# Two mixers on one core: where the norm's sum of squares is formed, and when its column product is issued

## The chip, the cores and the metric

The kernel runs on one core of a Trainium2 chip. The metric is the device time of one execution in microseconds (us), lower is better; the time before is the median of 3 runs. Engines are named as the profile names them: PE is TensorE (PEld its weight loads), DVE VectorE, ACT ScalarE, POOL GpSimd, SP the queue that issues most transfers.

## What is computed

`x` is (4, 1024, 512) float32, 4096 tokens of 512 features. Four residual stages follow each other, each on a layer norm of its input: mixer A, a feed-forward stage, mixer B, the same feed-forward stage again. Both mixers are state-space layers. Cut to what matters here, one of them is:

```
proj = x @ W_in                       # z (1024 wide), x/B/C (convolved over 4 taps, silu), dt
y    = scan over time per head, + D * x     # in tiles of 128 tokens, all in matmuls
A:  yf = y * silu(z);  out = (yf * rsqrt(mean(yf*yf) + eps) * norm_w) @ W_out
B:  out = (y * rsqrt(mean(y*y) + eps) * norm_w * silu(z)) @ W_out
```

The mean goes over the 1024 features of a token. Mixer A has 16 heads of width 64 and a state of 64, mixer B 64 heads of width 16 and a state of 128.

## The kernel before

`mixer_phase` is built once for each mixer. A step (a supertile in the code) is 256 tokens, two tiles of 128; there are 16 steps, 13 of them in a hardware loop. `FOLD` is true for mixer A alone (`2 * N == P`), and `NP` is 1 in A and 4 in B.

Features lie on the partitions: `yz[:, k, :]` holds features 128k to 128k+127 of a tile's 128 tokens, k from 0 to 7. The output is `yz` times `W_out`: 8 products of 128x512 that add up in one bank (L829). The norm's factor belongs to a token, so it is applied to the finished output (`out_add`, L1440), and what it needs is made in four parts:

- ACT squares `yz` (A) or the y bank (B) in two halves into `sq` (`square`, L1049).
- PE multiplies the eight blocks of `sq` by a matrix of ones (steps `rs0`, `prs`, L819): two products add up in each quarter of a bank's rows. DVE copies the bank to `rs` (`square_sums`, L1426).
- PE multiplies `rs` by the column `quad_row` (steps `rt0`, `prt`, L823): 128 sums, one for each token, in one column. DVE turns them into the variance (`rms_var`, L1430).
- ACT takes logarithm and exponential (`out_rsqrt`), and DVE adds a Newton step (`out_scale`, L93 to L95).

The even tile of a step does all that in the step's middle (`rs0`, `rt0`, `out0`); the odd tile's part is done in the head of the next step (`prs`, `prt`, `pout`), and the last odd tile's in an epilogue.

The order of each engine's work is written out by hand. For PE it is a list of names (`head`, `schedule`), and `run` issues them in turn. Every name that is no `seg`, `ydiag`, `ident` or `xT` uses one of the two `work` banks, alternately in the order of the list, and before it starts, `freed` waits until whoever reads the use two places before it is done:

```
if idx >= 2:
    freed(pe, sec.uses[idx - 2], i, n)
```

Around the change that means: `yoff0a/b` and `yoff1a/b` (L841, L845 in A, L800 in B: the part of y from the state) fill the two banks, DVE empties them in two operations (`from_state`, L1384), and the second of the two must be done before the output product in the bank of `yoffb` may start. `xnT0`, `xnT1` (L754) transpose the normalized x of the step after the next and are copied by ACT (`xnT_copy`, L958); `ident0` (L906) adds y1 to the y bank; `small1` (L791) makes exponents, `dt` (L759) needs both copies. After `pout`, DVE's `out_add` frees the bank for the use two places on. DVE's and ACT's orders are in their `supertile` functions. POOL adds the skip term to y1 after `from_state` (L1659), scales x (`xw`, L1670) and the state (L1676).

## Time and profile before

| what | value |
|---|---|
| median of 3 runs | 2761.14 us (2760.09 to 2762.21) |
| the profiled execution's own time | 2760.65 us |
| its span, first to last instruction | 2758.9 us |
| PE busy | 2678.3 us, 97% |
| DVE, ACT, POOL busy | 1962.0, 1530.8, 905.1 us |
| mean granted TensorE clock | 0.987 of full speed |

Mixer A takes the time from the start to about 1087 us, mixer B that from about 1300 to 2557 us, the two feed-forward stages the rest. The profile's times in a timeline are from the span's start. An fp32 product is two matmul instructions, so that a timeline counts 16 where the code has 8. Matmuls are pipelined: the time that a product takes in a stream is the distance from its start to the next one's, and the printed duration is longer. What bounds a stage is read from PE's idle time inside it and from the wait that ended it.

### The profile page before, as it was taken

What the parts mean: (1) busy time and instruction counts of PE and PEld (TensorE: products, weight loads), DVE (VectorE), ACT (ScalarE), POOL (GpSimd) and SP (SyncE); (2) the same over time, 40 slices, a digit from 0 to 9 for tenths busy, and PEclk for the clock granted to TensorE, in tenths of its full rate; (3) what the DMA queues carried; (4) which work ended last, traced back from release to release, by engine and by line L of the source; (5) the groups of instructions that cost most, each with busy time, mean ns of one, the idle gap of its engine ahead of it and who ended that gap; (6) DMA issues with size and microseconds to landing.
All of it is one profiled execution on the core that took longest, in us unless ns stands there. A gap on an engine that the chain in (4) does not pass through costs nothing. (4 is left out here: it accounts for less than half of the span.)

```text
span 2758.9 us, 49906 instructions
## 1 busy us (share of the span) xinstructions
PE 2678.3 (97%) x17452; PEld 1837.3 (67%) x17452; DVE 1962.0 (71%) x3701; ACT 1530.8 (55%) x2450; POOL 905.1 (33%) x611
## 2 busy tenths in 40 slices
PE   8999999999999999999999999999999999997998
PEld 7777777777777775356776666766677666773454
DVE  5666666666666655297788888888888888876377
ACT  4444444445444453343577677666677767765332
POOL 2222222223322223142333443334433344333144
PEclk8999999999999999999999999999999999998999
DMA  4000000000000005245000000000000000003433
GB/s 130 24 24 23 23 23 23 23 23 23 23 23 27 27 16 207 96 164 212 12 24 23 23 23 15 23 23 23 8 23 23 23 23 19 12 22 129 155 132 138
DMA packets 79994, 139.57 MB, mean 51 GB/s; under 512 B 17958, under 2 KB 17958, under 8 KB 78892
## 3 DMA queue, kind: packets, MB, share of 16 engines
q1 hardware_dynamic: 70812, 125.92, 13.1%
q10 hardware_dynamic: 9104, 12.63, 1.3%
q8 instruction: 47, 0.77, 0.1%
q14 instruction: 31, 0.25, 0.0%
HBM read 104.98 MB, written 33.55 MB: 50 GB/s over the span
## 5 line engine op out<-in xcount | busy, mean ns | idle before, releaser
L730 PE MATMUL work<-b_xnT,shared_w 128*128 128x256 f32 x2304 | 529.9, 384 | 1.9 <-DVE b_parts L1355 0.8
L730 PE MATMUL work<-a_xnT,shared_w 128*128 128x256 f32 x2176 | 497.4, 385 | 1.3
L730 PEld LDWEIGHTS work<-b_xnT,shared_w 128*128 128x128 f32 x2304 | 428.8, 190 | 76.4 <-issue 17.0
L730 PEld LDWEIGHTS work<-a_xnT,shared_w 128*128 128x128 f32 x2176 | 410.5, 191 | 70.3 <-issue 12.3
L1395 DVE TENSOR_TENSOR b_decay<-b_decay,b_gt 128x1024 f32<-128x1024 f32 x256 | 349.2, 1395 | 72.2 <-ACT b_decay L1039 71.6
L1032 ACT ACTIVATE b_decay<-seg 128x1024 f32<-128x1024 f32 x256 | 252.2, 1025 | 192.4 <-PE seg L872 184.5
L1624 POOL TENSOR_TENSOR b_rhs<-b_l_side,of_head 128x1024 fp32r<-128x1024 f32 x32 | 99.1, 3096 | 588.7 <-DVE b_l_side L1364 588.7
L1039 ACT ACTIVATE b_decay<-b_decay 128x1024 f32<-128x1024 f32 x256 | 263.6, 1066 | 0.0
L1659 POOL TENSOR_TENSOR a_y<-a_y,a_skip 128x1024 f32<-128x1024 f32 x32 | 90.0, 2813 | 473.1 <-DVE a_y L1384 473.1
L1274 DVE SCALAR_TENSOR_TENSOR shared_cv<-shared_pre,a_conv_w,shared_cv 128x256 f32<-128x256 f32 x432 | 189.8, 483 | 59.5 <-ACT shared_cv L974 53.8
L829 PE MATMUL work<-a_w_out,a_yz 128*128 128x512 f32 x512 | 228.4, 599 | 3.4 <-DVE a_y L1384 3.4
L829 PE MATMUL work<-b_w_out,b_yz 128*128 128x512 f32 x512 | 229.0, 600 | 0.5
L980 ACT COPY shared_z<-work 128x256 f32<-128x256 f32 (+1 forms) x192 | 84.6, 441 | 261.0 <-PE work L730 260.8
L1274 DVE SCALAR_TENSOR_TENSOR shared_cv<-shared_pre,b_conv_w,shared_cv 128x256 f32<-128x256 f32 x480 | 214.6, 481 | 18.0 <-ACT shared_cv L974 10.6
L973 ACT COPY shared_pre<-work 128x256 f32<-128x256 f32 x304 | 115.4, 380 | 165.5 <-PE work L730 165.5
L1395 DVE TENSOR_TENSOR a_decay<-a_decay,a_gt 128x1024 f32<-128x1024 f32 x64 | 137.9, 2175 | 84.2 <-ACT a_decay L1039 83.7
L829 PEld LDWEIGHTS work<-a_w_out,a_yz 128*128 128x128 f32 x512 | 95.4, 191 | 112.9 <-issue 108.1
L829 PEld LDWEIGHTS work<-b_w_out,b_yz 128*128 128x128 f32 x512 | 95.5, 192 | 110.4 <-issue 108.5
L886 PE MATMUL y<-b_decay,b_xdt 128*32 128x128 f32 x4096 | 129.4, 278 | 6.8 <-DVE b_decay L1395 6.7
L1659 POOL TENSOR_TENSOR b_y<-b_y,b_skip 128x1024 f32<-128x1024 f32 x32 | 82.9, 2590 | 154.3 <-DVE b_y L1384 154.3
L886 PEld LDWEIGHTS y<-b_decay,b_xdt 128*32 128x32 f32 x4096 | 107.9, 111 | 34.7 <-issue 21.8
L1881 PE MATMUL y<-f_x1T,shared_pre 128*128 128x512 f32 x256 | 123.6, 609 | 0.0
(330 smaller groups left out, 4563.6 us busy)
## 6 DMA issues: line engine op xcount, KB each, us to landing
x_mid<-mixer_x_res SPq DMA_DIRECT2D x64, 256.0 KB, 2.0
shared_x<-in_L_attn_a_x SPq DMA_DIRECT2D x16, 512.0 KB, 3.5
mixer_x_res<-in_L_attn_a_x SPq DMA_DIRECT2D x32, 256.0 KB, 2.6
shared_w<-in_L_ffn_d_w SPq DMA_DIRECT2D x2, 4096.0 KB, 13.5
f_d_w<-in_L_ffn_d_w SPq DMA_DIRECT2D x2, 4096.0 KB, 14.9
f_x_res<-x_mid SPq DMA_DIRECT2D x8, 1024.0 KB, 5.7
shared_x<-x_mid SPq DMA_DIRECT2D x16, 512.0 KB, 4.0
mixer_x_res<-x_mid SPq DMA_DIRECT2D x32, 256.0 KB, 2.6
```

The costliest lines, as they stand in the source:

```text
L730: mm = nc.tensor.matmul(dst, w_in[:, k, col:col + m], xnT[:, k, :], start=(k == 0), stop=(k == KD - 1))
L829: mm = nc.tensor.matmul(bank[:, :], yz[:, k, :], w_out[:, k, :], start=(k == 0), stop=(k == KE - 1))
L886: mm = nc.tensor.matmul(ybank[32 * q:32 * q + 32, slot * P:(slot + 1) * P], xdt[:, j, 4 * slot + q, 16 * odd:16 * odd + 32], decay[:, slot ...
L973: nc.scalar.copy(pre[0:m, b, HALO:], bank[0:m, 0:SUP])
L980: nc.scalar.copy(z_raw[:, got[0]:got[-1] + 1, :], sec.bank(name)[:, 0:len(got) * SUP].rearrange("p (b t) -> p b t", t=SUP)).then_inc(z_rea ...
L1032: nc.scalar.activation(decay[:, slot_buffer(j, s)].rearrange("p h l -> p (h l)"), seg[s % 2][:, :], ACT.Relu, scale=-1.0).then_inc(seg_tak ...
L1039: nc.scalar.activation(d, d, ACT.Exp, scale=-1.0).then_inc(exp_done, 1)
L1274: ins = nc.vector.scalar_tensor_tensor(out=cv[0:m, b, :], in0=pre[0:m, b, t:t + SUP], scalar=conv_w[0:m, b, t:t + 1], in1=cv[0:m, b, :], o ...
L1395: nc.vector.tensor_tensor(d, d, gt[:, j].unsqueeze(1).to_broadcast([P, 8, P]), ALU.mult).then_inc(m_ready, 1)
L1624: nc.gpsimd.tensor_tensor(rhs[1][:], l_side[:, 1].unsqueeze(1).to_broadcast([P, 8, P]), c["of_head"][:].unsqueeze(2).to_broadcast([P, 8, P ...
L1659: nc.gpsimd.tensor_tensor(y1[:], y1[:], skip[:], ALU.add).then_inc(y1x_ready, 1)
L1881: mm = nc.tensor.matmul(ybank[:, (m % 2) * 512:(m % 2 + 1) * 512], gate_w[:, k, m * P:(m + 1) * P], x1T[n][:, k, :], start=(k == 0), stop= ...
```

## The change

- Mixer A: the eight products with ones and DVE's copy are gone (`rs0`, `prs`). DVE adds the eight blocks of `sq` itself, with one reduction that reads `sq` with the block as the innermost axis (`add_squares`), and `rt0`, `prt` use a column of ones.
- Both mixers: `rt0` is no longer issued ahead of `out0`, but inside it, after the second of its eight products. In mixer A `prt` goes inside `pout` in the same way; in mixer B it stays where it was. The order of the bank uses is kept, so `out0` still waits for the second part of `from_state`.
- Mixer A, head of a step: PE's order after `seg0.0` was `prt, xnT0, pout, xnT1, ident0, small1` and is now `pout (prt inside), xnT0, ident0, xnT1, small1`. ACT squares the odd tile first of all instead of after `bt_copy`, and copies `xnT0` after the second exponential. DVE's reduction comes first, and `rms_var` after the second `make_xdt`.

```diff
@@ head(prev, nxt)
-                    + (["prs"] if prev else []) + ["yoff0a", "yoff0b", "seg0.0"] + (["prt"] if prev else [])
-                    + (["xnT0"] if nxt else []) + (["pout"] if prev else [])
-                    + (["seg0.1"] if NP > 1 else []) + (["xnT1"] if nxt else [])
-                    + ["ident0", "small1"])
+                    + (["prs"] if prev and not FOLD else []) + ["yoff0a", "yoff0b", "seg0.0"]
+                    + (["prt"] if prev else []) + (["xnT0"] if nxt and not FOLD else []) + (["pout"] if prev else [])
+                    + (["seg0.1"] if NP > 1 else []) + (["xnT0", "ident0"] if nxt and FOLD else [])
+                    + (["xnT1"] if nxt else []) + ([] if nxt and FOLD else ["ident0"]) + ["small1"])
@@ schedule, the part for NP == 1
-            steps += ["rs0", "yoff1a", "yoff1b", "seg1.0", "rt0", "out0"]
+            steps += ["yoff1a", "yoff1b", "seg1.0", "rt0", "out0"]
...
-        epi_steps = ["prs", "prt", "pout"]
+        epi_steps = ["prt", "pout"] if FOLD else ["prs", "prt", "pout"]
@@ use(name, sec)
-                        mm = nc.tensor.matmul(bank[:, 0:1], rs[:], c["quad_row"][:], start=True, stop=True)
+                        column = ones[:, 0:1] if FOLD else c["quad_row"][:]
+                        mm = nc.tensor.matmul(bank[:, 0:1], rs[:], column, start=True, stop=True)
...
                         for k in range(KE):
+                            if k == KE // 4 and (name == "out0" or FOLD):
+                                use("rt0" if name == "out0" else "prt", sec)
                             mm = nc.tensor.matmul(bank[:, :], yz[:, k, :], w_out[:, k, :],
@@ run(sec, steps)
-                            use(name, sec)
+                            if name != "rt0" and not (FOLD and name == "prt"):
+                                use(name, sec)
@@ ScalarE, supertile
+                    if prev and FOLD:
+                        square(2 * i - 1)
                     z_copy(sec, "zza")
...
-                    if prev:
+                    if prev and not FOLD:
                         square(2 * i - 1)
...
-                    if nxt:
+                    if nxt and not FOLD:
                         xnT_copy(sec, 0)
                     slot_exp(sec, 0, 1)
+                    if nxt and FOLD:
+                        xnT_copy(sec, 0)
@@ VectorE
+                def add_squares(tile):
+
+                    dve.wait_ge(sq_done, FREE + 2 * (tile + 1))
+                    nc.vector.tensor_reduce(rs[:], sq[:].rearrange("p b t -> p t b"), mybir.AxisListType.X, ALU.add
+                                            ).then_inc(rs_ready, 1)
@@ VectorE, supertile
+                    if prev and FOLD:
+                        add_squares(2 * i - 1)
                     masked_gt(sec)
                     make_xdt(sec, 0)
-                    if prev:
+                    if prev and not FOLD:
                         square_sums(sec, "prs")
                     from_state(sec, 0)
-                    if prev:
+                    if prev and not FOLD:
                         rms_var(sec, "prt")
                     make_xdt(sec, 1)
+                    if prev and FOLD:
+                        rms_var(sec, "prt")
...
-                    square_sums(sec, "rs0")
+                    add_squares(2 * i)
                     from_state(sec, 1)
```

PE, the head of a step of mixer A (`a_sq` squares, `a_state`/`a_bcs` the part from the state, `a_rs` the sums, `shared_x` the transposes `xnT`, `a_y` the product `ident0`, `a_aa` `small1`, `a_xnT` with 128x16 `dt`). Before:

```order
L819 MATMUL work<-a_sq,ones 32x128 x8
L841 MATMUL work<-a_state,a_bcs 128x256
L845 MATMUL work<-a_state,a_bcs 128x256
L841 MATMUL work<-a_state,a_bcs 128x256
L845 MATMUL work<-a_state,a_bcs 128x256
L872 MATMUL seg<-a_rhs,a_lhs 128x512 x4
L823 MATMUL work<-quad_row,a_rs 128x1
L754 MATMUL work<-ident,shared_x 128x128 x4
L829 MATMUL work<-a_w_out,a_yz 128x512 x8
L754 MATMUL work<-ident,shared_x 128x128 x4
L906 MATMUL y<-ident,a_y 128x128 x8
L791 MATMUL work<-tri_le,a_aa 64x128 x2
```

The same place in the changed kernel, whose lines are numbered a little higher:

```order
L844 MATMUL work<-a_state,a_bcs 128x256
L848 MATMUL work<-a_state,a_bcs 128x256
L844 MATMUL work<-a_state,a_bcs 128x256
L848 MATMUL work<-a_state,a_bcs 128x256
L875 MATMUL seg<-a_rhs,a_lhs 128x512 x4
L832 MATMUL work<-a_w_out,a_yz 128x512 x2
L824 MATMUL work<-ones,a_rs 128x1
L832 MATMUL work<-a_w_out,a_yz 128x512 x6
L754 MATMUL work<-ident,shared_x 128x128 x4
L909 MATMUL y<-ident,a_y 128x128 x8
L754 MATMUL work<-ident,shared_x 128x128 x4
L791 MATMUL work<-tri_le,a_aa 64x128 x2
```

The products with ones are gone, the column product sits inside the output products, the first transposes have moved behind these, and `ident0` stands ahead of the second transposes, which are now next to `small1`.

DVE, the same head. Before:

```order
L1345 TENSOR_TENSOR a_gt<-work,tri_le 128x256
L1328 TENSOR_TENSOR a_xdt<-a_xt,a_dt 128x1024
L1426 COPY a_rs<-work 128x128
L1384 TENSOR_TENSOR a_y<-work,a_e 128x512 x2
L1430 TENSOR_SCALAR a_rv<-work 128x1
L1328 TENSOR_TENSOR a_xdt<-a_xt,a_dt 128x1024
L1395 TENSOR_TENSOR a_decay<-a_decay,a_gt 128x1024
```

In the changed kernel:

```order
L1439 TENSOR_REDUCE a_rs<-a_sq 128x128
L1353 TENSOR_TENSOR a_gt<-work,tri_le 128x256
L1336 TENSOR_TENSOR a_xdt<-a_xt,a_dt 128x1024
L1392 TENSOR_TENSOR a_y<-work,a_e 128x512 x2
L1336 TENSOR_TENSOR a_xdt<-a_xt,a_dt 128x1024
L1444 TENSOR_SCALAR a_rv<-work 128x1
L1403 TENSOR_TENSOR a_decay<-a_decay,a_gt 128x1024
```

The copy became a reduction that waits for ACT alone and stands first; what follows `from_state` is now `make_xdt`, then the variance.

PE, the middle of a step of mixer B (`b_state` the part from the state, `b_w_out` the output products), in the changed kernel:

```order
L800 MATMUL work<-b_state,b_bcs 128x512 x2
L875 MATMUL seg<-b_rhs,b_lhs 128x512 x4
L832 MATMUL work<-b_w_out,b_yz 128x512 x2
L824 MATMUL work<-quad_row,b_rs 128x1
L832 MATMUL work<-b_w_out,b_yz 128x512 x6
```

Before, the row with `b_rs` stood between `seg` and the eight output products; nothing else moved there.

## Rows read from the trace of the kernel before

**Rows 1.** Busy time by engine in mixer A's and mixer B's loops (start:end, length, PE, PEld, DVE, ACT, POOL, clock, DMA).
```profile
120.00:880.00 760.00, 748.70 (x4361) 547.06 (x4360) 487.79 (x1010) 368.62 (x662) 221.91 (x136) 1.00 0.07 24
1400.00:2300.00 900.00, 897.10 (x6984) 629.68 (x6984) 743.56 (x1224) 639.92 (x966) 334.65 (x165) 1.00 0.06 20
```
**Rows 2.** Timeline of PE, middle of a step of mixer A (start us, length us, ...).
```profile
486.33 0.64 PE L819 MATMUL work<-a_sq,ones 128*32 128x128 f32 x16
486.90 0.70 PE L841 MATMUL work<-a_state,a_bcs 64*128 64x256 f32 x2
...
488.88 0.38 PE L823 MATMUL work<-quad_row,a_rs 128*128 128x1 f32 x2
489.48 1.98 PE L829 MATMUL work<-a_w_out,a_yz 128*128 128x512 f32 x4 [0.21 <-DVE a_y L1384]
```
**Rows 3.** Timeline of DVE at the same place.
```profile
487.04 0.29 DVE L1426 COPY a_rs<-work 128x128 f32<-128x128 f32 x1 [1.92 <-PE work L819]
488.14 1.29 DVE L1384 TENSOR_TENSOR a_y<-work,a_e 128x512 f32<-128x512 f32 x2 [0.80 <-PE work L841]
```
**Rows 4.** Timeline of ACT at the same place.
```profile
484.56 1.23 ACT L1049 ACTIVATE a_sq<-a_yz 128x512 f32<-128x512 f32 x2 [3.69 <-DVE a_yz L1420]
...
486.44 0.37 ACT L980 COPY shared_z<-work 128x256 f32<-128x256 f32 x1 [0.39 <-PE work L730]
```
**Rows 5.** Timeline of PE, head of the next step of mixer A.
```profile
515.75 0.65 PE L819 MATMUL work<-a_sq,ones 128*32 128x128 f32 x16
...
519.47 7.03 PE L829 MATMUL work<-a_w_out,a_yz 128*128 128x512 f32 x16
526.34 0.60 PE L754 MATMUL work<-ident,shared_x 128*128 128x128 f32 x4
526.77 1.04 PE L906 MATMUL y<-ident,a_y 128*128 128x128 f32 x8
527.89 0.44 PE L791 MATMUL work<-tri_le,a_aa 128*64 128x128 f32 x4
528.26 1.96 PE L759 MATMUL work<-shared_w,a_xnT 128*128 128x16 f32 x16
530.07 2.19 PE L730 MATMUL work<-a_xnT,shared_w 128*128 128x256 f32 x9
```
**Rows 6.** DVE's reductions over 128 and over 64 elements, by source line.
```profile
L332 DVE TENSOR_REDUCE of_head<-hd x1: 286/286/286, 6.6 to 6.6; 128x8 f32<-128x128 f32 x1
L333 DVE TENSOR_REDUCE low_row<-low x1: 210/210/210, 6.8 to 6.8; 128x1 f32<-128x64 f32 x1
```
**Rows 7.** Timeline of DVE in the same head.
```profile
517.55 1.29 DVE L1384 TENSOR_TENSOR a_y<-work,a_e 128x512 f32<-128x512 f32 x2 [0.80 <-PE work L841]
...
522.85 2.35 DVE L1395 TENSOR_TENSOR a_decay<-a_decay,a_gt 128x1024 f32<-128x1024 f32 x1 [2.80 <-ACT a_decay L1039]
...
527.10 0.74 DVE L1440 SCALAR_TENSOR_TENSOR mixer_x_res<-work,a_rr,mixer_x_res 128x512 f32<-128x512 f32 x1
```
**Rows 8.** Timeline of POOL in the same head.
```profile
522.21 1.90 POOL L1670 TENSOR_TENSOR a_xw<-a_xdt,a_e 128x1024 f32<-128x1024 f32 x1
```
**Rows 9.** Timeline of ACT in the same head: the copy of the second transposes.
```profile
526.97 0.59 ACT L958 COPY a_xnT<-work 128x512 f32<-128x512 f32 x1 [2.49 <-PE work L754]
```
**Rows 10.** Timelines of ACT and DVE, last step of mixer A and its epilogue.
```profile
1058.63 1.23 ACT L1049 ACTIVATE a_sq<-a_yz 128x512 f32<-128x512 f32 x2 [7.65 <-DVE a_yz L1420]
...
1062.65 1.29 DVE L1384 TENSOR_TENSOR a_y<-work,a_e 128x512 f32<-128x512 f32 x2 [1.65 <-PE work L841]
...
1086.34 2.94 ACT L232 ACTIVATE shared_z<-shared_z,ffn_shift,ffn_r_in 128x512 f32<-128x512 f32 x4 [5.74 <-POOL ffn_shift L226]
```
**Rows 11.** Timelines of PE and DVE, middle of a step of mixer B.
```profile
1915.33 0.38 PE L823 MATMUL work<-quad_row,b_rs 128*128 128x1 f32 x2
1915.75 7.13 PE L829 MATMUL work<-b_w_out,b_yz 128*128 128x512 f32 x16
...
1915.00 0.69 DVE L1384 TENSOR_TENSOR b_y<-work,b_e 128x512 f32<-128x512 f32 x1 [0.17 <-PE work L800]
```

More of the change, by code:

```diff
@@ L1611, in _ @@
                 sec = epilogue()
-                square_sums(sec, "prs")
+                if FOLD:
+                    add_squares(2 * NSUP - 1)
+                else:
+                    square_sums(sec, "prs")
                 rms_var(sec, "prt")
```

## The prediction

> **What bounds the kernel now.** I read first the busy time by engine inside the two mixers' loops [rows 1]: PE works 748.7 of 760 us in mixer A and 897.1 of 900 us in mixer B, at a granted clock of 1.00, while DVE, the next one, is at 488 and 744 us. So what counts is the start of each PE product, and the question at every edit is whether a removed or moved product leaves PE working or waiting. That is read from the timelines around the output products, one step of each mixer, since the steps of a loop repeat.
>
> In the middle of a step of A [rows 2] the products with ones hold PE for 486.90 - 486.33 = 0.57 us. Then come the part from the state, `seg`, and the column product at 488.88. The output products start at 489.48, after 0.21 us of idling that DVE's second y1 ended: it ran 488.14 + 1.29 = 489.43 [rows 3]. Remark this: **the output product waits for y1, and the column product before it is done inside that wait**. In mixer B it is the same to the hundredth, though the profile prints no idle time there: the second y1 ends at 1915.00 + 0.69 = 1915.69, the output products start at 1915.75, and the column product at 1915.33 fills the 0.42 us before [rows 11].
>
> **What the change costs and gives, part by part.**
>
> *The price of a column product in the stream.* Inside the output products nothing covers it but its first weight load. The nearest row is `dt`, 16 instructions with only 16 columns and full weights, from 528.26 to 530.07 [rows 5]: 0.113 us each, so 0.23 us for the two of a column product. The bounds are 0.1 (only one of the two loads shows) and 0.42 (what it takes alone, [rows 11]). I take 0.23, because the operation is the same and the streams alike.
>
> *DVE's reduction.* It reads 1024 elements. Reductions over 128 and over 64 elements took 0.286 and 0.210 us [rows 6]: 0.0012 us an element, so 0.29 + 896 x 0.0012 = 1.35 us. An operation over 2 x 512 elements took 1.29 [rows 3]. I take 1.3; the bounds are 1.1 and, because these rows read neighbouring elements and the new one jumps 512 bytes from element to element, twice the estimate, 2.6.
>
> *Even tile of A.* The squares end at 484.56 + 1.23 = 485.79 [rows 4], so the reduction runs 485.85 to 487.15, where DVE idled 1.92 us for PE [rows 3]. On PE the part from the state moves to 486.33. Its second product needs the other bank, now freed by ACT's copy at 486.44 + 0.37 = 486.81 [rows 4] instead of by DVE's copy at 487.04 + 0.29 = 487.33 [rows 3]. That is 0.52 us earlier, and with it go `seg` and both y1: the first y1 would start at 487.62, and the reduction is done before. The output products start 0.52 earlier and take 0.23 more: **-0.29 us**. The 0.57 us of products is thus given back almost by half, since the column product leaves its cover. 15 such tiles: -4.4 us.
>
> *Odd tile of A, in the next head.* Again everything up to y1 moves up by 0.53, from 518.84 to 518.31 [rows 7]. ACT's squares and DVE's reduction are done before the head's first products end. The output products start at 518.36; they took 526.34 - 519.47 = 6.87 [rows 5], and 0.23 more now, to 525.46. `xnT0` adds 0.43 and `ident0` 0.9 (the printed 1.04 is pipelined, the transposes go at 0.11 to 0.12 an instruction), to 526.8. Now `xnT1` stands in the place two behind `pout` and waits for DVE's `out_add`, as `small1` did before. In the old trace `out_add` ended at 527.10 + 0.74 = 527.84 and `small1` started at 527.89 [rows 5, 7]: DVE's chain was the bound there already. What sets it: the first slot product of DVE took 2.35 us, although 1.2 is enough; it ended at 525.20, 1.1 us after POOL's `xw` at 522.21 + 1.90 = 524.11 [rows 7, 8]. Whatever the reason, DVE came through when POOL was done, and POOL's chain starts from y1, 0.5 us earlier now. So `out_add` ends about 0.55 earlier, 527.25. `xnT1` starts at 527.30, 0.5 us late. And behind it there is only `small1` to cover ACT's copy: before, that copy began 526.97 - 526.34 = 0.63 after the transposes' start and took 0.59 [rows 9]. So `dt` starts at 527.30 + 0.63 + 0.59 + 0.05 = 528.57, against 528.26 [rows 5]: **+0.31 us**. 14 heads: +4.4 us. The first step's head has no `pout`, but `dt` also comes behind the later `xnT1`: +0.5, once.
>
> *Last step of A.* PE has no projections left there, and the chain runs over the squares, the sums and y1. The squares end at 1058.63 + 1.23 = 1059.86; with a reduction of 1.3 y1 starts at 1061.2 instead of 1062.65 [rows 10]: -1.45. Its head gives another -0.3. Behind the epilogue, the next stage waits for ACT's normalization, 1086.34 + 2.94 = 1089.28 [rows 10], which hangs on DVE's last Newton step; 0.57 us of products and a copy of 0.29 with their handovers are exchanged for 1.3 us of reduction: 0.
>
> *Mixer B.* The output product still waits for the second y1, so it starts at 1915.75 as before, and the column product now costs its 0.23 inside. **+0.23 us** for each of 16 even tiles, PE being full: +3.7. `rms_var` comes 1.7 us later, but ACT, which waits for it, has two exponentials to do first.
>
> Sum: -4.4 + 4.4 + 0.5 - 1.45 - 0.3 + 0 + 3.7 = **+2.4 us** on the profiled execution's own 2760.65, which lies 0.49 under the median of the runs. On the median: 2761.14 + 2.4 = **2763.5 us**. About 0.2%, 5.5 us, is what a measurement of this kernel can tell from no change.
>
> **The rivals.**
>
> *The reduction is slow.* It may take up to 1.8 us before y1 of the even tile is late (487.62 - 485.85). At 2.6 it costs 0.8 in each of 15 even tiles, and 1.3 each in the last step and the epilogue: +14.6, so 2778. For it speaks only that no row reads with such a jump; against it, that the rows of DVE, whatever they read, are all near 1.2 ns an element.
> The Trainium skill ("SBUF — State Buffer", in the section "Door 1: The DMA port swizzle") says that each access to a new 16-byte line pays a penalty, so that float32 can be strided only 4 elements for free; every element of this reduction is on a new line. No row here shows it; if it holds for VectorE, this rival is the outcome.
>
> *The head is worse: DVE's chain does not move up with POOL.* Then `out_add` still ends at 527.84, `xnT1` starts at 527.89 and `dt` at 529.16: +0.9 instead of +0.31, 14 times, +8.3 more: 2771.8, slower. It decides from an `out_add` that moves less than 0.3 us. For it: the slot product also waits for ACT's exponential, whose start the change doesn't move.
>
> *The head is free.* If `out_add` ends by 526.8, `dt` is bound by the transposes alone and starts at about 528.05: -0.2 instead of +0.31, 14 times, -7.1: 2756.4, just inside no change. DVE would have to gain a full microsecond.
>
> *PE's busy time is what counts.* Removed are 32 x 0.57 = 18.2 us of an engine that is 98 to 99% busy; if the waits I found give way too, nearly all of it comes back: 2761 - 18 + 4 = 2747. Against it stands that each of these products is followed by a wait for y1 [rows 2], which the change only shifts.
>
> **How the numbers follow.** Forecast 0.52, slow reduction 0.08, worse head 0.16, free head 0.14, full gain 0.10. Of the forecast's share I give 0.04 to slower, 0.03 to faster, since +-0.25 us in one head is +-3.5 us, and 0.1 to 0.42 for the column product is another -4 to +6; of the free head's 0.05 is faster. So faster 0.18, slower 0.28, same 0.54. The range runs from the free head to the worse one, 2756 to 2771.8, and leaves out the slow reduction and the full gain, 0.18 together.
>
> **What would show it.** In the new profile: the reduction at 1.2 to 1.4 us; the output products of A's even tile starting within 0.1 us of the end of y1; a column product of 0.2 to 0.25 us between the second and third output product; in A's head an idle time of some 0.5 us before the second transposes, ended by `mixer_x_res` of DVE, and another of 0.2 to 0.4 before `dt`, ended by ACT's copy; a step of A as long as before, a step of B 0.23 us longer. The prediction is wrong if a step of A is shorter by more than 0.3 us, or if the time of B does not grow.

## The result, and the profile after

The changed kernel takes **2784.02 us** (median of 4 runs, 2783.32 to 2784.55); the kernel before, run beside it, 2761.68 (2760.09 to 2763.30). The ratio is 1.008, 95% interval 1.0064 to 1.0096: slower by 0.8%, where I had forecast 2763.5 and a range up to 2771.8. The profiled execution's span is 2782.8 us, against 2758.9.

Busy time by engine in the two loops, changed kernel, the columns of [rows 1]:
```profile
120.00:880.00 760.00, 734.50 (x3896) 533.08 (x3895) 492.49 (x977) 363.39 (x645) 231.61 (x136) 0.98 0.07 24
1400.00:2300.00 900.00, 893.53 (x6962) 625.47 (x6961) 741.99 (x1217) 640.78 (x959) 336.23 (x166) 1.00 0.06 21
```
Mixer B looks as before. In mixer A PE is busy 14 us less; since both windows are 760 us long, that says that it waits 14 us more, not that it has 14 us less to do. Beside it **the granted clock is 0.98 instead of 1.00**. To see where, I took the distance from one step's `sums` products (three small ones, issued once in a step) to the next one's (start to start, us):
```
            before                  changed kernel
mixer A     58.78, then 14 x 65.87  59.54, 66.09, 67.76, 67.78, 67.77, 66.09, 67.77, 67.78,
                                    66.08, 67.76, 67.77, 67.77, 66.08, 67.77, 67.70
mixer B     74.33, 76.68,           77.36, 76.92,
            12 x 76.80, 77.47       12 x 77.02, 77.71
```
Every step of A is 0.22 us longer, and 10 of the 14 another 1.68 us (the expectations below say 11; it is 10). Two neighbouring heads of the changed kernel in PE's timeline show what the 1.68 us are:
```profile
402.06 1.93 PE L759 MATMUL work<-shared_w,a_xnT 128*128 128x16 f32 x16 [0.40 <-ACT a_xnT L962]
403.84 15.79 PE L730 MATMUL work<-a_xnT,shared_w 128*128 128x256 f32 x72
...
468.15 1.93 PE L759 MATMUL work<-shared_w,a_xnT 128*128 128x16 f32 x16 [0.40 <-ACT a_xnT L962]
469.93 17.47 PE L730 MATMUL work<-a_xnT,shared_w 128*128 128x256 f32 x72
```
The same 72 projections take 15.79 us behind one head and 17.47 behind the next. The windows of 10 us behind these two heads have the clock in the third column from the right:
```profile
404.00:414.00 10.00, 10.00 (x47) 8.81 (x48) 5.81 (x17) 4.67 (x12) 0.00 (x0) 1.00 0.09 24
...
470.00:480.00 10.00, 10.00 (x40) 8.52 (x40) 4.11 (x13) 3.82 (x10) 0.00 (x0) 0.83 0.08 25
471.00:473.00 2.00, 2.00 (x6) 1.56 (x6) 0.76 (x4) 0.06 (x1) 0.00 (x0) 0.50 0.06 20
```
PE is busy in all of both, but in the second the clock is 0.83 on average: a part of it ran at the lower level, 1.2 GHz (the last row, 0.50), the rest at 2.4, and 17% of 10 us are lost, which is the 1.7 us. Such a stretch is called a *fall* from here on. All ten begin 1.8 to 2.8 us behind the start of `dt`, in the first microsecond of the projections. What PE did in the 60 us before, waits and all, is the same to 0.02 us in both.

**The balance of the 24 us of span**, from the starts of the `sums` products:

- mixer A's steps: 14 x 0.22 = +3.1; 10 falls x 1.68 = +16.8; the first step +0.76; what comes before it -1.67; last step and epilogue -0.76. Together +18.1: the next stage starts at 1107.67 instead of 1089.58.
- the stage between gives 0.4 back.
- mixer B: 14 x 0.22 and 0.24 in the last step, +3.2 with rounding; and its first step +3.0.

The last is not the change's. PE waits long in that step in both kernels, and the clock falls there in both (0.84 from 1321 to 1345 before, 0.67 from 1352 to 1373 in the changed one), but where it falls varies. In the kernels below, some of which have B exactly as before, the same step took 74.68 to 77.4 us; the 74.33 of before is the lucky end of that. The -1.67 ahead of A's first step isn't the change's either: the work up to there is the same in all these kernels, and it ended between 42.9 and 45.9 us. Nor is the +0.76 of the first step shown to be: it took 59.40 in the kernel with the reduction alone below, whose head is the old one. So of the 24 us 17 are falls behind A's heads, 3 and -1.7 are chance, and the rest is some 6.

PE's timeline of the changed kernel at the two places of [rows 2, 5], even tile and head:
```profile
493.74 0.70 PE L844 MATMUL work<-a_state,a_bcs 64*128 64x256 f32 x2
...
496.38 1.98 PE L832 MATMUL work<-a_w_out,a_yz 128*128 128x512 f32 x4 [0.55 <-DVE a_y L1392]
498.21 0.28 PE L824 MATMUL work<-ones,a_rs 128*128 128x1 f32 x2
498.35 5.40 PE L832 MATMUL work<-a_w_out,a_yz 128*128 128x512 f32 x12
503.58 3.62 PE L730 MATMUL work<-a_xnT,shared_w 128*128 128x256 f32 x16
...
522.88 0.70 PE L844 MATMUL work<-a_state,a_bcs 64*128 64x256 f32 x2
...
525.50 1.98 PE L832 MATMUL work<-a_w_out,a_yz 128*128 128x512 f32 x4 [0.53 <-DVE a_y L1392]
...
532.70 0.60 PE L754 MATMUL work<-ident,shared_x 128*128 128x128 f32 x4
533.13 1.04 PE L909 MATMUL y<-ident,a_y 128*128 128x128 f32 x8
534.51 0.65 PE L754 MATMUL work<-ident,shared_x 128*128 128x128 f32 x4 [0.34 <-DVE mixer_x_res L1454]
535.09 0.44 PE L791 MATMUL work<-tri_le,a_aa 128*64 128x128 f32 x4
535.93 1.93 PE L759 MATMUL work<-shared_w,a_xnT 128*128 128x16 f32 x16 [0.40 <-ACT a_xnT L962]
537.70 7.54 PE L730 MATMUL work<-a_xnT,shared_w 128*128 128x256 f32 x26
```
There are now four waits in a step: 0.55 and 0.53 ahead of the output products, 0.34 ahead of the second transposes, 0.40 ahead of `dt`. And DVE's and ACT's rows there, which answer to [rows 3, 7, 9]:
```profile
493.23 1.91 DVE L1439 TENSOR_REDUCE a_rs<-a_sq 128x128 f32<-128x1024 f32 x1 [0.70 <-ACT a_sq L1053]
495.05 1.28 DVE L1392 TENSOR_TENSOR a_y<-work,a_e 128x512 f32<-128x512 f32 x2
...
533.64 0.74 DVE L1454 SCALAR_TENSOR_TENSOR mixer_x_res<-work,a_rr,mixer_x_res 128x512 f32<-128x512 f32 x1
...
535.20 0.59 ACT L962 COPY a_xnT<-work 128x512 f32<-128x512 f32 x1 [1.28 <-PE work L754]
```

### The profile page after: what moved, and what is told of

Read it like the earlier page. It is cut to its first block and busy times, and to the rows that moved or that the text cites. A ratio compares the mean times of both kernels' runs of the same rounds, so it can differ in the third digit from the quotient of the medians.

```text
span 2782.8 us, 48759 instructions
## 1 busy us (share of the span) xinstructions
PE 2675.2 (96%) x16940; PEld 1833.7 (66%) x16940; DVE 1995.6 (72%) x3701; ACT 1533.0 (55%) x2450; POOL 916.4 (33%) x611
## 5 line engine op out<-in xcount | busy, mean ns | idle before, releaser
L730 PE MATMUL work<-a_xnT,shared_w 128*128 128x256 f32 x2176 | 513.2, 394 | 1.3
L730 PEld LDWEIGHTS work<-a_xnT,shared_w 128*128 128x128 f32 x2176 | 421.6, 197 | 75.0 <-issue 12.3
L832 PE MATMUL work<-a_w_out,a_yz 128*128 128x512 f32 x512 | 237.0, 607 | 20.4 <-DVE a_y L1392 19.5
L1403 DVE TENSOR_TENSOR a_decay<-a_decay,a_gt 128x1024 f32<-128x1024 f32 x64 | 117.2, 1852 | 38.0 <-ACT a_decay L1043 35.9
```

The lines of the kernel that those rows point to most:

```text
L730: mm = nc.tensor.matmul(dst, w_in[:, k, col:col + m], xnT[:, k, :], start=(k == 0), stop=(k == KD - 1))
L832: mm = nc.tensor.matmul(bank[:, :], yz[:, k, :], w_out[:, k, :], start=(k == 0), stop=(k == KE - 1))
L1403: nc.vector.tensor_tensor(d, d, gt[:, j].unsqueeze(1).to_broadcast([P, 8, P]), ALU.mult).then_inc(m_ready, 1)
```

## The experiments

Three theories. T1: the clock falls because PE waits in A's new head, and what counts is where it waits. T2: it falls with the reduction, or because PE has less to do. T3: it has nothing to do with the waits. The kernel before ran beside each batch, at 2761 to 2762; ratios are against it. Step lengths are of mixer A unless said.

### One part undone at a time

**Head order back.** The changed kernel, with the head's order of before on PE, which also puts the head's column product ahead of `pout` again (the one inside `out0` stays):
```diff
-                    + (["prt"] ...) + (["xnT0"] if nxt and not FOLD else []) + (["pout"] if prev else [])
-                    + (["seg0.1"] ...) + (["xnT0", "ident0"] if nxt and FOLD else [])
-                    + (["xnT1"] ...) + ([] if nxt and FOLD else ["ident0"]) + ["small1"])
+                    + (["prt"] ...) + (["xnT0"] if nxt else []) + (["pout"] if prev else [])
+                    + (["seg0.1"] ...) + (["xnT1"] if nxt else []) + ["ident0", "small1"])
...
-                            if k == KE // 4 and (name == "out0" or FOLD):
-                                use("rt0" if name == "out0" else "prt", sec)
+                            if k == KE // 4 and name == "out0":
+                                use("rt0", sec)
...
-                            if name != "rt0" and not (FOLD and name == "prt"):
+                            if name != "rt0":
```


> The changed kernel with TensorE's order in mixer A's head put back (column product, first transposes, output products, second transposes, ident0, small1); the reduction and the column product inside out0 stay. In the changed kernel a step of A takes 66.09 us, or 67.77 us where the granted clock falls behind dt (11 of 14 steps). Theory 1 (the head's new waits, 0.33 us ahead of the second transposes and 0.40 us ahead of dt, together with 0.53 us ahead of the output products, let the clock fall): with two of the three waits gone no step shows a lower clock, and a step takes 65.87 - 0.28 (even tile) - 0.53 (head) = 65.06 us; the whole some 2752 us. Theory 2 (the reduction on VectorE or the 0.54 us wait in the even tile is what lets the clock fall): most steps keep a fall, 1.7 us each, and the whole is some 2770 us. Theory 3 (the fall has nothing to do with TensorE's waits): the number of falls stays at 11.

Measured: 2761.81 us, ratio 0.9999 (0.9990 to 1.0009). All 14 steps took 65.64 or 65.65, none fell; B 77.02 a step. So with the old head the falls are gone, and 22 us with them. The step is 0.6 longer than expected, for a wait I had not seen. PE's timeline of this kernel:
```profile
516.76 0.65 PE L754 MATMUL work<-ident,shared_x 128*128 128x128 f32 x4 [0.22 <-DVE a_y L1392]
517.88 7.13 PE L832 MATMUL work<-a_w_out,a_yz 128*128 128x512 f32 x16 [0.47 <-DVE a_rv L1444]
```
`pout` waited for `rms_var`, which the change put behind `make_xdt` on DVE. That wait of 0.47 us, longer than `dt`'s 0.40 in the changed kernel, brought no fall.

**Columns ahead.** The changed kernel, with the column products in their own place again, in both mixers:
```diff
                         for k in range(KE):
-                            if k == KE // 4 and (name == "out0" or FOLD):
-                                use("rt0" if name == "out0" else "prt", sec)
...
-                            if name != "rt0" and not (FOLD and name == "prt"):
-                                use(name, sec)
+                            use(name, sec)
```


> The changed kernel with the column products of both mixers ahead of the output products again; the reduction and the new head order stay. Mixer B: a step goes back from 77.02 to 76.80 us in any theory that prices the column product at 0.22 us in the stream and at nothing in the wait for y1. Mixer A: the even tile gains 0.22 us, the head nothing, since it is bound by out_add; a step without a fall of the clock takes 65.87 us. Theory 1: the waits ahead of the output products shrink from 0.53 to 0.2 us, but the one ahead of the second transposes grows to 0.55 us; fewer falls than 11, some 2761 to 2770 us. Theory 3: 11 falls, 2776 us.

Measured: 2775.79 us, ratio 1.0051 (1.0034 to 1.0068). B 76.80 a step, that is 0.22 less than in the changed kernel; A 65.87 without and 67.55 with a fall, 8 falls. The waits ahead of the output products shrink to 0.21, those in the head stay (0.56 and 0.40), and so do most falls. The time is T3's number, but with 8 falls and not 11; T1's range, up to 2770, was missed.

**The reduction alone.** The kernel before, with only the reduction in place of the products with ones, and ACT's squares early in the head; the column products stay ahead, the head's order and `rms_var`'s place stay old:
```diff
-            steps += ["rs0", "yoff1a", "yoff1b", "seg1.0", "rt0", "out0"]
+            steps += ["yoff1a", "yoff1b", "seg1.0", "rt0", "out0"]
...
-                    square_sums(sec, "rs0")
+                    add_squares(2 * i)
... (the same for the odd tile and the epilogue, with the column of ones and the early squares)
```


> The kernel before with the reduction on VectorE in place of the products with ones in mixer A, ScalarE's early squares included, and nothing else: column products ahead, head's order as before. Theory 1: no fall of the clock; both tiles gain what y1 gains, 0.5 us each, so a step of A takes 64.8 us, and the whole some 2746 us: faster than before. Theory 2 (the reduction itself, or the lower share of work on TensorE, lets the clock fall): 1.7 us for each step with a fall, up to 2765 us. Mixer B as before, 76.80 us a step.

Measured: **2748.07 us, ratio 0.9951 (0.9934 to 0.9968), faster than before**. All 14 steps took 64.90 (the last 64.83), no fall; B 76.80. PE does as little here as in the changed kernel, with the same reduction: T2 falls. Its timeline in the even tile and the head:
```profile
482.93 7.13 PE L830 MATMUL work<-a_w_out,a_yz 128*128 128x512 f32 x16 [0.21 <-DVE a_y L1387]
...
512.39 7.03 PE L830 MATMUL work<-a_w_out,a_yz 128*128 128x512 f32 x16
519.26 0.60 PE L754 MATMUL work<-ident,shared_x 128*128 128x128 f32 x4
519.69 1.04 PE L907 MATMUL y<-ident,a_y 128*128 128x128 f32 x8
520.88 0.44 PE L791 MATMUL work<-tri_le,a_aa 128*64 128x128 f32 x4 [0.15 <-DVE mixer_x_res L1449]
521.25 1.96 PE L759 MATMUL work<-shared_w,a_xnT 128*128 128x16 f32 x16
```
`dt` has no wait: the products of `ident0`, which stand behind the second transposes here, cover ACT's copy.

**The head's order alone.** The kernel before with the new head order on PE, and ACT's later copy, and nothing else:
```diff
-                    + (["xnT0"] if nxt else []) + (["pout"] if prev else [])
-                    + (["seg0.1"] if NP > 1 else []) + (["xnT1"] if nxt else [])
-                    + ["ident0", "small1"])
+                    + (["pout"] if prev else []) + (["seg0.1"] ...) + (["xnT0", "ident0"] if nxt else [])
+                    + (["xnT1"] if nxt else []) + ["small1"])
```


> The kernel before with the head's new order for TensorE (output products, first transposes, ident0, second transposes, small1) and ScalarE's later copy of the first transposes in mixer A, and nothing else: products with ones and column products as before, no reduction. A wait of some 0.7 to 0.8 us ahead of the second transposes (out_add is not earlier here) and 0.40 us ahead of dt; a step without a fall takes 65.87 + 1.0 us, where the order before had no such waits. Theory 1 (TensorE's waits in the head make the clock fall): falls of 1.7 us in many steps, 2785 us or more. Theory 2 (the reduction or the removed products have a part in it): no falls, 2776 us.

Measured: 2804.32 us, ratio 1.0152 (1.0135 to 1.0169), the slowest of all. The steps took 68.65 (11 of 14) or 70.3 (3): a fall in every one, 66.97 + 1.68 by my reckoning since none is without, and in three one of twice the length. PE's timeline:
```profile
544.91 0.65 PE L754 MATMUL work<-ident,shared_x 128*128 128x128 f32 x4 [0.64 <-DVE mixer_x_res L1442]
...
546.33 1.93 PE L759 MATMUL work<-shared_w,a_xnT 128*128 128x16 f32 x16 [0.40 <-ACT a_xnT L958]
```
No reduction is needed for falls; the new order brings them by itself. That it brings more of them than the changed kernel because its waits are longer is not shown: "columns ahead", with 0.56 and 0.40 in the head, has 8, the changed kernel, with 0.34 and 0.40, has 10. Its cost without them is 66.97 - 65.87 = 1.10 us a step.

### The waits filled

If T1 holds, a kernel that does *more* must be faster. In the next five kernels two more identity products (0.5 to 0.6 us of PE, into a bank that is free) stand in some of the waits of a step; they compute nothing that is used.
```diff
+                def filler(bank, count):
+                    for _ in range(count):
+                        nc.tensor.matmul(bank[:, 0:P], ident[:], ident[:], start=True, stop=True)
...
+                            if FOLD and name in ("xnT1", "dt") and "pout" in sec.uses and "xnT1" in sec.uses:
+                                pe.wait_ge(seg_taken, FREE + 2 * sec.i * NS + 2)
+                                filler(seg[0], 2)
```
This is the one that fills the head's two waits. Ahead of the output products the two go into the `work` bank that the column product uses next; the rest differs in the names.

**All four.**

> The changed kernel with two products of the identity with itself (0.45 us) put into each of the four waits of a step of A: ahead of both output products, ahead of the second transposes and ahead of dt. They compute nothing. Theory 1: TensorE no longer stands still there, the clock does not fall, every step takes 66.1 to 66.4 us, the whole some 2766 to 2770 us, 15 to 18 us faster than the changed kernel although it does more. Theory 3: the falls stay, 2784 us or more.

Measured: 2767.83 us, ratio 1.0022 (1.0012 to 1.0031). All 14 steps took 66.10, no fall. That is **16 us less than the changed kernel with more work**: T3 falls. The filled waits in PE's timeline:
```profile
527.35 0.61 PE L916 MATMUL seg<-ident 128*128 128x128 f32 x4
527.85 0.65 PE L754 MATMUL work<-ident,shared_x 128*128 128x128 f32 x4
528.43 0.44 PE L791 MATMUL work<-tri_le,a_aa 128*64 128x128 f32 x4
528.80 0.71 PE L916 MATMUL seg<-ident 128*128 128x128 f32 x4
529.35 1.86 PE L759 MATMUL work<-shared_w,a_xnT 128*128 128x16 f32 x16
```
**Only the two ahead of the output products.**

> The changed kernel, only the two waits ahead of the output products filled with two identity products each; the head's waits of 0.33 and 0.40 us stay. If the falls of the clock come from all waits together, there are fewer than 11 but some; if from the head's two waits alone, 11 falls stay, 2784 us; if from the waits ahead of the output products, none, 2767 us.

Measured: 2783.76 us, ratio 1.0078 (1.0061 to 1.0095), 9 falls: as the changed kernel.

**Only the head's two.**

> The changed kernel, only the waits ahead of the second transposes and of dt filled; the waits of 0.53 us ahead of the output products stay. If the head's waits make the clock fall, none is left: steps of 66.1 us, 2767 us. If the waits ahead of the output products do, 11 falls stay, 2784 us.

Measured: 2767.79 us, ratio 1.0023 (1.0013 to 1.0032), no fall, though both waits of 0.5 us stay.

**Only the one ahead of the second transposes.**

> The changed kernel with only the wait of 0.33 us ahead of the second transposes filled. With both of the head's waits filled there was no fall of the clock in 13 steps. If that wait is the decisive one, no fall, steps of 66.1 us, 2768 us; if it is dt's wait of 0.40 us, about 10 falls, 2784 us; if it is the sum of both, falls in some steps, between.

Measured: 2783.54 us, ratio 1.0076 (1.0059 to 1.0093), 10 falls: as the changed kernel.

**Only the one ahead of `dt`.**

> The changed kernel with only the wait of 0.40 us ahead of dt filled: the counterpart. If dt's wait is decisive, no fall and 2768 us; if the one of the transposes, about 10 falls and 2784 us.

Measured: 2771.56 us, ratio 1.0034 (1.0021 to 1.0046), 2 falls. PE's timeline of it:
```profile
597.91 0.71 PE L916 MATMUL seg<-ident 128*128 128x128 f32 x4
598.46 1.86 PE L759 MATMUL work<-shared_w,a_xnT 128*128 128x16 f32 x16
600.17 15.79 PE L730 MATMUL work<-a_xnT,shared_w 128*128 128x256 f32 x72
```
Filling these 0.40 us takes 8 of 10 falls away, filling the 0.34 beside them none, and both together all ten. So `dt`'s wait decides, and the other adds a little to it. These five can be compared fall by fall, since a step without a fall takes 66.1 us in each of them, as in the changed kernel.

### The reduction's layout

**Blocks innermost.** The kernel with the reduction alone, with the squares laid out so that DVE reads neighbours and ACT writes with a step of 32 bytes:
```diff
-        sq = sb("sq", [P, KE, P])
+        sq = sb("sq", [P, P, KE]) if FOLD else sb("sq", [P, KE, P])
```


> Reduction alone, with the squares stored so that the eight blocks of a token lie next to each other: VectorE's reduction reads neighbouring elements, and ScalarE writes with a step of 32 bytes. Theory S (the step of 512 bytes is what makes the reduction 1.91 us instead of the 1.3 us estimated): it takes 1.2 to 1.35 us. Theory R (a reduction with 128 outputs of 8 elements costs that much wherever it reads): it stays at 1.9 us. ScalarE's squares may grow from 0.63 us each. The time moves little either way, since the reduction with 1.91 us ends just when y1 can start: 2746 to 2749 us.

Measured: 2762.61 us, ratio 1.0004 (0.9994 to 1.0013), 14.5 us above the kernel it is made from and far outside what I expected. The tiles `a_rs` and `a_sq` (ns: shortest, median, longest):
```profile
L1435 DVE TENSOR_REDUCE a_rs<-a_sq x32: 1219/1220/1221, 90.6 to 1077.7; 128x128 f32<-128x1024 f32 x32
L1051 ACT ACTIVATE a_sq<-a_yz x64: 1120/1142/1174, 88.5 to 1076.6; 128x512 f32<-128x512 f32 x64
```
In the changed kernel the reduction took
```profile
L1439 DVE TENSOR_REDUCE a_rs<-a_sq x32: 1893/1913/1961, 90.0 to 1095.6; 128x128 f32<-128x1024 f32 x32
```
The stride costs DVE 0.69 us, as I had thought. But ACT's two squares now take 1.14 each instead of 0.63, its `z` copy comes late, and PE waits for it:
```profile
486.61 0.47 PE L842 MATMUL work<-a_state,a_bcs 64*128 64x256 f32 x1 [0.57 <-ACT shared_z L981]
```
The steps took 65.40, or 67.10 in 4 of them. So there are falls with the old head too, once other waits come: T1 in its narrow form, that only the new head brings them, doesn't hold. Two of the four lie where the new wait is, in the even tile's output products just behind it; PE's timeline of one tile without a fall and one with it:
```profile
158.71 7.13 PE L830 MATMUL work<-a_w_out,a_yz 128*128 128x512 f32 x16 [0.21 <-DVE a_y L1388]
...
224.12 8.83 PE L830 MATMUL work<-a_w_out,a_yz 128*128 128x512 f32 x16 [0.21 <-DVE a_y L1388]
```
The other two lie behind `dt`, although the head waits no longer than in the kernel with the reduction alone.

### The wait shortened

In DVE's timeline of the changed kernel `out_add` (L1454) stands behind the second slot product, 1.32 us, which nobody needs as early. Two kernels put it ahead:
```diff
                         out_scale(2 * i - 1)
+                    if prev and FOLD:
+                        out_add(sec, "pout", i - 1, 1)
                     slot_mult(sec, 0, 1)
-                    if prev:
+                    if prev and not FOLD:
                         out_add(sec, "pout", i - 1, 1)
```
**In the changed kernel.**

> The changed kernel, in mixer A's head VectorE adds the odd tile's output ahead of the second slot product instead of behind it. out_add then ends some 0.8 us earlier (output products end, 0.75 us of addition), before ident0 is done, so the wait of 0.33 us ahead of the second transposes goes, the 0.40 us ahead of dt stays. A step without a fall takes 65.8 us. Falls as in the run that fills that wait alone; the whole 2762 to 2765 us without falls, 2780 us with them.

Measured: 2768.29 us, ratio 1.0025 (1.0015 to 1.0035). 65.53 a step, 67.22 in 5. PE's timeline:
```profile
527.78 0.60 PE L754 MATMUL work<-ident,shared_x 128*128 128x128 f32 x4
...
529.14 1.93 PE L759 MATMUL work<-shared_w,a_xnT 128*128 128x16 f32 x16 [0.40 <-ACT a_xnT L962]
```
The wait ahead of the transposes is gone; `dt`'s, which comes from the head's own order, stays, and half of the falls with it. The time lies between the two that I expected: the kernel with only the transposes' wait filled has the same four waits (0.55, 0.53, 0, 0.40) and 10 falls.

**With the reduction alone** (old head, columns ahead).

> Reduction alone (the version that beat the kernel before), with out_add ahead of the second slot product as well. small1 there starts 0.15 us late because of out_add; that wait goes: 64.75 instead of 64.90 us a step, 2 us in all, 2746 us. Rival: the slot product comes 0.75 us later and delays something unseen, then no gain or a loss.

Measured: **2744.38 us, ratio 0.9935 (0.9919 to 0.9952)**: the best of all, 17 us under before. 64.68 a step, no fall.

PE's waits in mixer A from 120 to 1000 us in groups (sum, count, longest) show the difference without a timeline. Before:
```profile
PE work L754 <- DVE a_y L1384: 4.0, 14, 0.3
PE work L808 <- ACT shared_z L980: 4.0, 13, 0.3
PE work L829 <- DVE a_y L1384: 2.8, 13, 0.2
PE work L791 <- DVE mixer_x_res L1440: 0.2, 1, 0.2
```
The changed kernel:
```profile
PE work L832 <- DVE a_y L1392: 14.6, 27, 0.6
PE work L759 <- ACT a_xnT L962: 5.2, 13, 0.4
PE work L754 <- DVE mixer_x_res L1454: 4.3, 13, 0.3
PE work L808 <- ACT shared_z L984: 4.0, 13, 0.3
```
The waits sum to 28 us instead of 11, and the third and second group are new: those of the head. All kernels by their waits in one step (us; the one at L808, 0.31, stands in each) and their falls in the 14 steps:
```
kernel                    xnT0   out0   pout   xnT1   small1 dt     falls
before                    0.29   0.21   0      0      0      0      0
reduction alone           0.22   0.21   0      0      0.16   0      0
same, out_add first       0.22   0.21   0      0      0      0      0
head order back           0.22   0.56   0.47   0      0      0      0
all four filled           0      0      0      0      0      0      0
head's two filled         0      0.55   0.53   0      0      0      0
dt's filled               0      0.55   0.53   0.34   0      0      2
blocks innermost          0.22   0.22*  0      0      0.16   0      4
changed, out_add first    0      0.55   0.53   0      0      0.40   5
columns ahead             0      0.21   0      0.56   0      0.40   8
out and pout filled       0      0      0      0.34   0      0.40   9
xnT1's filled             0      0.55   0.53   0      0      0.40   10
changed                   0      0.55   0.53   0.34   0      0.40   10
head order alone          0      0.21   0.21   0.64   0      0.40   14
* and 0.57 ahead of the part from the state, 0.16 ahead of the column product
```
With `dt`'s wait there are 5 to 14 falls, without it 0 to 4. The sum of the waits does not order them: 1.25 us in "head order back" brings none, 1.17 in "columns ahead" brings 8. The falls are counted in one execution of each kernel; the times of its other executions differ from that one by up to 3.5 us, in "head order alone" by up to 4.1, so a count is good to some two falls.

The falls don't come at random either. In the changed kernel they go 3, 2, 3, 2 with one step without between them, and with two heads of the same waits ("changed, out_add first" and "xnT1's filled") it is 5 falls at 65.53 us a step and 10 at 66.09. So a count depends on the length of the step too, and only kernels with equal steps, the five filled ones and the changed kernel, show what a wait is worth.

## Why the prediction was wrong

**Where the products' starts go, the forecast held.**

- *A column product in the stream*, 0.23 forecast. B's step grew by 0.22 and lost it again with the columns ahead. Right.
- *Even tile of A*, -0.29 forecast. From the part from the state to the projections behind the output products it is 503.58 - 493.74 = 9.84 us; before, where the products with ones came first, 10.12 from their start at 486.33 [rows 2]: -0.28. Right, though the reduction took 1.91 instead of 1.3. By my working y1 could start 1.29 us behind the part from the state, at 495.03; it started at 495.05, as the reduction ended: the slack was just used up.
- *Head*, +0.31 forecast. From the part from the state to the projections 537.70 - 522.88 = 14.82, against 530.07 - 515.75 = 14.32 from the products with ones before [rows 5]: +0.50. The mechanism is right. `out_add` came 0.59 earlier, forecast 0.55. What was too small are the handovers: 0.13 from `out_add` to the transposes and 0.14 from ACT's copy to `dt`, where I had 0.05 each; the copy began 0.69 behind the transposes' start, not 0.63.
- *First step's head*, +0.5 forecast. The step grew by 0.76, but no run shows that the head is the reason (59.40 with the old head in "reduction alone", against 58.78 before).
- *Last step and epilogue*, -1.75 forecast, -0.76 measured. From the end of the squares to y1 it is 1079.96 - 1078.11 = 1.85 us, against 2.79 [rows 10]: -0.94. In the epilogue I had exchanged 1.3 us of reduction evenly; it took 1.89. The mis-sized term is the reduction's, twice 0.6 us.

With the measured sizes the sum would be 14 x 0.22 + 16 x 0.22 + 0.76 - 0.76 = +6.6 us, 2767.7, well in the range; nothing but the clock carries it out.

**The step that failed** is the reading of [rows 1] with which the prediction begins: it takes "at a granted clock of 1.00" as a property of the loop, and so the sum has no term for the clock at all. I foresaw both waits of the head (0.5 and 0.2 to 0.4; they are 0.34 and 0.40) and priced them at their own length, 0.31 us together. What they cost is 0.50 us in each step, and in 10 of 14 steps 1.68 us more in the projections behind them, because the clock falls to 1.2 GHz in them. That is 16.8 of the 24 us, and none of my four rivals had it. The prediction names what would make it wrong: a shorter step of A, or a B that doesn't grow. Neither happened; I had not asked what would make A's step *longer*, although the clock stood in a column of the rows that I quoted.

**The rivals.** *The reduction is slow* was the nearest to the truth of the reduction: 1.91 us, between my 1.3 and its 2.6. The Trainium skill ("SBUF — State Buffer", section "Door 1: The DMA port swizzle") says that an access that moves to a new 16-byte line pays a penalty; the traces agree as far as they go, by the pair 1.91 and 1.22 us for DVE's reads and 1.14 and 0.63 us for ACT's writes. That the line has 16 bytes no run shows: the steps tried are 4, 32 and 512. My argument against, that all rows of DVE are near 1.2 ns an element, rested on rows that all read neighbours. Its price, some 14 us, did not come about, since PE's path in the even tile had the 1.8 us of slack that I had worked out. *The head is worse* did not come about in its own mechanism. *PE's busy time counts* did not come about: some 18 us of products are gone and the time rose, and PE's busy time over the whole kernel hardly fell (2675.2 us, before 2678.3), since a product takes longer in a fall. But a part of it was there to be had, as the reduction alone shows: 65.87 - 64.90 = 0.97 us a step, when the column products stay in their cover and the head keeps its order.

**Part by part**, then, against the time before in the same batch: the reduction in place of the products with ones is worth -14 us (2748.07); the columns inside cost 0.22 a tile; the new head, where only it is changed, costs 1.10 a step by its waits and, with them, the falls. The whole is +22; the parts don't add up to it exactly, since in the changed kernel `out_add` comes earlier and the head costs less.

## What stays open

Why the changed kernel has a fall behind some heads and not behind others, whose products lie the same to 0.02 us, no run here settles: heads that look alike are not alike to the clock. The regular order of the falls suggests that it also matters when a head comes, and not only what is in it; no kept trace shifts a head in time without changing it, so that stays untested, and with it how far "reduction alone" owes its 0 falls to the length of its step (4 executions, all within 2 us, speak against chance). Nor is it shown why `dt`'s wait weighs more than a longer one ahead of `pout`. What is special in its place is what can be read: the products around it are the short ones (`small1` 0.44, the transposes 0.65, `dt` 1.93 us for 16 products of 16 columns), and behind it come the long projections, in which the fall then lies. And "blocks innermost" has 2 falls behind `dt` without any new wait in the head.

## What to carry to other kernels

A wait of 0.4 us on an engine that is 97% busy can cost four times its length, in the work behind it: look at the granted clock of the loop before and after, and list the lengths of the steps, since a mean hides that some are 1.68 us longer. When a reorder removes the short products that cover a copy (here `ident0` from behind the second transposes), price the wait that it bares with and without a fall; if the engine must wait, a product that computes nothing in its place can be the cheaper choice. And try the parts of a change alone: here one of them is worth -14 us, with `out_add` moved as well -17, and the whole is +22.

## What the runs showed of the hardware that I had not expected

- The clock of a PE that is 97% busy (734.5 of 760 us) fell from 2.4 to 1.2 GHz behind groups of waits of 0.2 to 0.6 us; each fall cost 1.68 us where it lay over full work. Two identity products in a wait of 0.40 us took 8 of 10 falls away.
- The place of a wait counted more than its length: 0.56 and 0.47 us ahead of the output products brought no fall, 0.40 ahead of `dt` did, and so did 0.57, 0.16 and 0.21 us within 3 us of each other ahead of the even tile's output products.
- A reduction over 1024 float32 took 1.91 us with 512 bytes from element to element and 1.22 with neighbours. Written with a step of 32 bytes, ACT's squares of 512 elements took 1.14 instead of 0.63 us, so the layout moved the cost to an engine where it hurt more.
- A column product of two instructions costs 0.22 us inside a stream of 128x512 products; alone it is listed with 0.38 and starts 0.4 us ahead of what follows.
